# Two attention layers on one NeuronCore: the gated layer between them and the second attention merged into one block, with its first units interleaved, and the turned maxima spread by ScalarE in four scaled pieces

## The chip, the cores and the metric

The kernel runs on one core of a Trainium2 chip. The metric is the device time of one execution in microseconds (us), of which the median of several runs is quoted. A profile is one further execution taken with the hardware profiler. Engines: TensorE (PE; its weight loads are listed apart as PEld), VectorE (DVE), ScalarE (ACT), GpSimd (POOL) and the queue of SyncE (SP). Each works through its own list of instructions in order and meets the others at semaphores.

## What is computed

The input is 2048 tokens of 128 features. Two layers follow each other, each of the form `x = x + attention(norm(x)) * silu(ffn(norm(x)))`, all in fp32. What the change touches is the end of the first layer and the start of the second:

```python
x = x + s * g                       # end of layer 0
xn = _layernorm(x, axis=-1)
s = _L1_attn_ref(xn, W_Q, W_K, W_V, W_O, b_Q, b_K, b_V, b_O)   # 16 heads of 64, causal softmax
g = _silu(_L1_ffn_ref(xn, w_gate, w_up, w_down))               # silu(gate) * up, then down; int8 weights
x = x + s * g
```

Sequence and batch in the second attention: one sequence of 2048 tokens, 16 heads. The scores of a token are shifted by their row maximum before the exponential.

## The kernel before, in words

The program is a chain of blocks: loading and routing, the first attention, `between` (L1260) and `attention1` (L1536). A block ends with all engines meeting.

**Sizes.** Tokens are cut into 4 chunks of 512 (`C`) and 16 tiles of 128. PSUM has 8 banks of 128x512 fp32. The 16 heads of the second attention are done as 8 head pairs, each head on 64 of the 128 partitions.

**`between`** computes the gated layer of layer 1 and, at its start, finishes the last chunk of layer 0. For each chunk: `turn_xn` (L1316) transposes the normalised tokens, ScalarE copies them out twice (`take_xn`, L1396 and L1397: a rounded high part and the full one), VectorE takes the low part (`take_low`, L1459). `gate(c, f)` (L1333) is four matmuls for one third of the hidden columns; its number is n = 3c + f and it has one of two pairs of banks, so it waits for product n - 2. ScalarE does the Silu (L1404), VectorE the product (`multiply`, L1465), and `down(c)` (L1345) is 24 matmuls over the three products of the chunk, whose Silu ScalarE writes to `g` (L1412). Chunk 3 is late, since its tokens are the last of layer 0: its join (projection L1369, `join_sum`, moments, variance, a Sqrt on ScalarE L1392, `join_refine`, and on GpSimd `join_result` L380 to L384 and `join_normal` L390) runs beside the other chunks, twice a Sqrt between Silus. `down(3)` ends the block.

**`attention1`** is a fixed list of units, which PE fills and another engine takes out of its banks, in the same order on all queues (`fill` on PE, `take` on ScalarE and VectorE). Kinds of unit:
- project (L1780 to L1782): six matmuls to two banks, keys and queries of a head pair for a chunk. ScalarE writes the high parts with the bias (L1941, L1943), VectorE the low parts (L2016, L2020).
- maximum (L1806, L1811): a tile of 128 query rows against one chunk of keys, both heads, two banks. VectorE reduces each bank (L2030); after the last tile of a chunk a small reduction writes the negated maxima (L2037).
- turn (L1818): these maxima transposed, one bank. They are then spread into `max_rows` (L2044 on VectorE): each of the chunk's four tiles of columns is the turned 128x128 matrix times `own_tile`, which is one on the rows of that tile and zero on the others.
- scores (L1859, L1862): a chunk of queries against a tile of keys, both heads, with the maxima added by a matmul of ones against `max_rows`; the first scores of a chunk wait for its turn unit to be taken. ScalarE does the exponential, one instruction (L1968) where the two banks are neighbours, two (L1972) where they wrap round.
- value (L1793 to L1795), mix (L1840), total (L1828), bias (L1889).

Seven banks form a ring, given out in the order of the list, one or two at a time; a unit waits until the earlier owner of its bank has been taken. The eighth bank collects the weighted values (`weigh`, L1881). The list has 80 groups: each has four scores units with maximum tiles between them (counts in `MAXIMA`: 8, 6, 6, 8, 8 and then 2 to 5), after them the units of `STARTING` or `WHOLE` (projections, turns, values, mixes), then the total of a chunk that has ended, and last the four weighings of the group's scores. ScalarE copies a chunk's sum out (L1980), VectorE divides (reciprocal L2051, product L2054), and after the mix adds to the accumulator `attn` (L2103); in the last head pair it also multiplies by `g` and adds `x` (`finish`, L2006 and L2007). GpSimd sums the exponentials (L1763, L1765, L1769) and masks the diagonal (L1737).

In front of the groups stands `BEFORE`, one list for all engines:

```python
BEFORE = [("project", 0, 0), ("project", 0, 1)] + TILES[0:TC] + [("value", 0, 0), ("turn", 0, 0), ("bias", 0, 0)]
```

Before it the biases are turned (L1913), ScalarE copies them (L1931) and rounds the value weights (L1933), and GpSimd takes their low part (L1729), for which the value units wait. The bias unit is 16 matmuls; VectorE adds it to `row_o` (L2114) and spreads the row over all 16 tiles of `attn` (L2116), then starts the reductions of group 0.

## Time and profile before

| | us |
|---|---|
| median of 3 runs (lowest, highest) | 1384.57 (1384.45, 1385.58) |
| the profiled execution, its time | 1383.88 |
| its span, first to last instruction | 1381.9 |
| PE / DVE / ACT / POOL busy in the span | 1292.8 / 1024.9 / 755.8 / 691.7 |
| mean granted TensorE clock | 0.991 |
| start of `between` | 499.70 |
| last down projection of `between` | 531.99 |
| first scores of `attention1` | 547.74 |
| first weighing | 559.52 |

Dates are microseconds from the span's start. The clock is given as a share of the full 2.4 GHz; at 0.5 TensorE runs at 1.2 GHz. In a timeline row, several instructions of one kind are merged (x8), the second number is their time together, and the bracket says how long the engine had stood before and for whom. A group row gives the busy sum and the mean of one.

### The profile page before, as it was taken

What the parts mean: (1) busy time and instruction counts of PE and PEld (TensorE: products, weight loads), DVE (VectorE), ACT (ScalarE), POOL (GpSimd) and SP (SyncE); (2) the same over time, 40 slices, a digit from 0 to 9 for tenths busy, and PEclk for the clock granted to TensorE, in tenths of its full rate; (3) what the DMA queues carried; (4) which work ended last, traced back from release to release, by engine and by line L of the source; (5) the groups of instructions that cost most, each with busy time, mean ns of one, the idle gap of its engine ahead of it and who ended that gap; (6) DMA issues with size and microseconds to landing.
All of it is one profiled execution on the core that took longest, in us unless ns stands there. A gap on an engine that the chain in (4) does not pass through costs nothing. (4 is left out here: it accounts for less than half of the span.)

```text
span 1381.9 us, 26461 instructions
## 1 busy us (share of the span) xinstructions
PE 1292.8 (94%) x9840; PEld 677.4 (49%) x9840; DVE 1024.9 (74%) x1818; ACT 755.8 (55%) x1286; POOL 691.7 (50%) x528
## 2 busy tenths in 40 slices
PE   5889999999999987989999999999999999999897
PEld 3763222222222246555555655555655555655554
DVE  7667888888888875776766766766767766676868
ACT  6476777778887864344444444444444444444343
POOL 4101050100101111558787678777688787778771
PEclk9899999999999999999999999999999999999999
DMA  1522410000000000000000000000000000000000
GB/s 36 180 101 80 126 29 1 2 1 1 1 2 1 2 1 1 1 1 1 1 1 1 1 1 1 1 1 2 1 1 1 1 1 1 1 1 1 9 9 16
DMA packets 18172, 21.56 MB, mean 16 GB/s; under 512 B 7785, under 2 KB 15873, under 8 KB 16513
## 3 DMA queue, kind: packets, MB, share of 16 engines
q1 hardware_dynamic: 18048, 19.88, 4.5%
q8 instruction: 83, 1.36, 0.4%
q14 instruction: 41, 0.33, 0.1%
HBM read 14.63 MB, written 5.24 MB: 14 GB/s over the span
## 5 line engine op out<-in xcount | busy, mean ns | idle before, releaser
L1769 POOL TENSOR_TENSOR acc<-acc,prob 128x1024 f32<-128x1024 f32 (+3 forms) x250 | 493.8, 1975 | 87.0 <-ACT prob L1968 53.1
L2030 DVE TENSOR_REDUCE part_max<-psum 128x1 f32<-128x512 f32 (+3 forms) x640 | 352.8, 603 | 143.1 <-PE psum L1806 71.9
L1968 ACT ACTIVATE prob<-psum 128x1024 f32<-128x1024 f32 (+3 forms) x273 | 241.7, 896 | 285.7 <-PE psum L1862 279.9
L695 DVE TENSOR_SCALAR w<-psum 128x512 f32<-128x512 f32 x472 | 304.5, 686 | 59.3 <-PE psum L544 46.5
L644 ACT ACTIVATE w<-psum 128x512 f32<-128x512 f32 x552 | 293.9, 601 | 81.7 <-PE psum L544 81.3
L564 PE MATMUL psum<-w,v_cols 128*32 128x512 f32 x2048 | 274.0, 608 | 0.0
L1881 PE MATMUL psum<-prob,v_both 128*64 128x512 f32 (+3 forms) x1280 | 250.2, 533 | 0.6 <-POOL prob L1737 0.6
L1859 PE MATMUL psum<-q_hi,k_hi 64*128 64x512 f32 (+3 forms) x640 | 135.6, 408 | 32.0 <-DVE part_max L2030 17.7
L1881 PEld LDWEIGHTS psum<-prob,v_both 128*64 128x64 f32 x1280 | 87.7, 137 | 145.4 <-issue 134.6
L1806 PE MATMUL psum<-k_hi,q_hi 64*128 64x512 f32 (+3 forms) x640 | 135.7, 411 | 5.2 <-DVE part_max L2030 2.6
L1859 PE MATMUL psum<-q_lo,k_hi 64*128 64x512 f32 (+3 forms) x640 | 122.8, 364 | 0.0
L1862 PE MATMUL psum<-max_rows,ones_r 64*128 64x512 f32 (+3 forms) x640 | 122.6, 363 | 0.0
L1859 PE MATMUL psum<-q_hi,k_lo 64*128 64x512 f32 (+3 forms) x640 | 122.5, 363 | 0.0
L544 PEld LDWEIGHTS psum<-q_rows,k_rows 32*128 32x128 f32 x768 | 40.2, 181 | 153.9 <-ACT w L644 148.1
L2051 DVE RECIPROCAL inv<-psum 128x512 f32<-128x512 f32 x31 | 103.9, 3352 | 13.2 <-PE psum L1828 12.8
L380 POOL TENSOR_SCALAR xa<-xa,rstd_j,shift_j 128x128 f32<-128x128 f32 x16 | 6.9, 448 | 199.4 <-DVE shift_j L372 199.4
L1806 PEld LDWEIGHTS psum<-k_hi,q_hi 64*128 64x128 f32 x640 | 65.0, 184 | 83.0 <-issue 75.6
L1737 POOL TENSOR_SCALAR_AFFINE_SELECT prob<-prob 128x256 f32<-128x256 f32 x128 | 53.2, 423 | 97.6 <-ACT prob L1968 89.1
L544 PE MATMUL psum<-q_rows,k_rows 32*128 32x512 f32 x768 | 101.4, 493 | 0.1
L1859 PEld LDWEIGHTS psum<-q_hi,k_hi 64*128 64x128 f32 x640 | 65.9, 186 | 64.8 <-issue 49.4
L1765 POOL TENSOR_TENSOR acc<-prob 128x1024 f32<-128x1024 f32 x23 | 55.0, 2390 | 37.8 <-ACT prob L1968 32.3
L1972 ACT ACTIVATE prob<-psum 128x512 f32<-128x512 f32 (+3 forms) x94 | 45.5, 537 | 51.6 <-PE psum L1862 50.3
(310 smaller groups left out, 1486.4 us busy)
## 6 DMA issues: line engine op xcount, KB each, us to landing
q_rows<-q_dram SPq DMA_DIRECT2D x12, 256.0 KB
k_rows<-k_dram SPq DMA_DIRECT2D x3, 1024.0 KB
x<-in_L_attn_x SPq DMA_DIRECT2D x4, 256.0 KB, 3.8
mask<-in_L_ffn_attention_mask SPq DMA_DIRECT2D x1, 1024.0 KB, 5.9
q_dram<-x_high SPq DMA_DIRECT2D x1, 1024.0 KB, 6.9
q_dram<-x_low SPq DMA_DIRECT2D x1, 1024.0 KB, 6.9
k_dram<-q_rows SPq DMA_DIRECT2D x1, 1024.0 KB, 9.0
k_dram<-k_rows SPq DMA_DIRECT2D x1, 1024.0 KB, 6.2
```

The lines of the kernel that those rows point to most:

```text
L544: last = nc.tensor.matmul(pair_bank[n % RING][i], k_rows[group][rows, kt * P:(kt + 1) * P], q_rows[group][rows, qc * C:(qc + 1) * C], star ...
L564: last = nc.tensor.matmul(out_bank[turn % 2][h * VW:(h + 1) * VW, :], v_cols[group][:, kt, h, :], w[:, s % WR, h, :], start=(kt == 0), sto ...
L644: nc.scalar.activation(w[:, s % WR, 2 * m + i, :], pair_bank[n % RING][i], ACT.Relu)\
L695: nc.vector.tensor_scalar(w[:, s % WR, 2 * m + 1, :], pair_bank[n % RING][1], 0.0, None, ALU.max)\
L1769: nc.gpsimd.tensor_tensor(sums, sums, prob[:, s % PR, :, q0:C], ALU.add).then_inc(summed, 1)
L1806: last = nc.tensor.matmul(to[m][:, 0:n], q_hi[HALF[m], i * P:(i + 1) * P], k_hi[hp % 2][HALF[m], c * C:c * C + n], start=True, stop=not di ...
L1859: nc.tensor.matmul(to[m][:, q0:C], left[HALF[m], keys], right[HALF[m], at], start=n == 0, stop=False)
L1862: last = nc.tensor.matmul(to[m][:, q0:C], ones_r[HALF[m], :], max_rows[HALF[m], at], start=False, stop=True)
L1881: last = nc.tensor.matmul(out_bank[HALF[m], q0:C], v_pair[hp % 2][:, kt, HALF[m]], prob[:, s % PR, m, q0:C], start=kt == 0, stop=kt == (qc ...
L1968: last = nc.scalar.activation(prob[:, s % PR, :, q0:C], sh.psum[:, first:first + 2, q0:C], ACT.Exp, scale=SCALE)
L2030: free(nc.vector.tensor_reduce(part_max[:, m, i, c:c + 1], src[m][:, 0:cols], AX_X, ALU.max), unit, m)
L2051: free(nc.vector.reciprocal(inv[:, :], banks_of(unit)[0]), unit, 0)
```

## The change

The two blocks become one, `between_and_attention1`, with the buffers of the one laid over those of the other where they are free. Nine units that stood behind the block's end are put between the gates and down projections of the middle part, with fixed banks (`EARLY`): the bias unit (bank 3), projections (0,0) and (0,1), the first four maximum tiles (banks 2 and 3) and the first turn (bank 2). Only value unit (0,0) stays in `BEFORE`; the ring begins there at place 4. The turned biases go through bank 2 at the start, and the banks of the middle part are dealt out anew. VectorE's reductions and low parts, and ScalarE's high parts, stand in the matching places of their queues. The rounding of the value weights moves on ScalarE behind `take_xn(3)`. The spread of the bias row over `attn` moves from VectorE to GpSimd, behind the join and the last `turn_xn`, in front of the low value weights; value units wait for both, VectorE's groups for the spread. Last, `spread_maxima` of all 32 turn units moves from VectorE (one product of 128x512 with `own_tile`) to ScalarE (four copies of 128x128, each scaled by a column of `own_tile`).

```diff
-def attention1(nc, a, sh, out):
+def between_and_attention1(nc, a, sh, out):
...
-        BEFORE = [("project", 0, 0), ("project", 0, 1)] + TILES[0:TC] + [("value", 0, 0), ("turn", 0, 0), ("bias", 0, 0)]
+        EARLY = [(("bias", 0, 0), [3]), (("project", 0, 0), [2, 3])] + [(tile, [2, 3]) for tile in TILES[0:TC]] \
+            + [(("turn", 0, 0), [2]), (("project", 0, 1), [2, 3])]
+        BEFORE = [("value", 0, 0)]
         LAST = [("total", FINAL, None), ("mix", NP - 1, NC - 1)]
         HALVES = 2
-        UNIT = BEFORE + [u for k in range(GROUPS) for u in units_of(k)] + LAST
+        UNIT = [u for u, _ in EARLY] + BEFORE + [u for k in range(GROUPS) for u in units_of(k)] + LAST
         AT = {u: n for n, u in enumerate(UNIT)}
         WIDE = ("scores", "maximum", "project", "value")
         BANKS, EARLIER, FREED = {}, {}, {}
-        held, freed, place = [None] * RING, [0] * RING, 0
+        held, freed, place = [None] * RING, [0] * RING, 4
         for u in UNIT:
-            width = 2 if u[0] in WIDE or u == LAST[-1] else 1
-            BANKS[u] = [(place + i) % RING for i in range(width)]
-            place += width
+            if u in dict(EARLY):
+                BANKS[u] = dict(EARLY)[u]
+            else:
+                width = 2 if u[0] in WIDE or u == LAST[-1] else 1
+                BANKS[u] = [(place + i) % RING for i in range(width)]
+                place += width
             EARLIER[u] = [held[b] for b in BANKS[u]]
             for b in BANKS[u]:
...
-        q_hi = sb("q_hi", [P, S], F32R)
+        q_hi = sh.q_rows[1]
         q_lo = sb("q_lo", [P, S], F32R)
-        k_hi = [sb(f"k_hi{n}", [P, S], F32R) for n in range(2)]
+        k_hi = [sh.k_rows[1], sb("k_hi1", [P, S], F32R)]
         k_lo = [sb(f"k_lo{n}", [P, S], F32R) for n in range(2)]
         max_rows = sb("max_rows", [P, S], F32R)
-        v_both = sb("v_both", [P, 2, T, P])
+        v_both = sh.v_both
...
+        inner = prob[:, :, :, :].rearrange("p n m c -> p (n m c)").rearrange("p (f s) -> p f s", s=S)
+        act_gate = acc[:, 0, :, :]
+        wT = z[:, 0, 0:F1]
+        wT_int = k_hi[1][:, 0:2 * F1].rearrange("p (m f) -> p m f", f=F1)
+        w_real = v_both[:, 0, 0:3 * F1T, :].rearrange("p t d -> p (t d)").rearrange("p (m f) -> p m f", f=F1)
+        oT = v_both[:, 1, 0:TC, :].rearrange("p t d -> p (t d)")
...
+        gate_bank = [bank[4:6], bank[6:8]]
+        last_bank = bank[6 + TURN % 2]
+        ROWS_BANK = [0, 1, 2, 0]
+        JOIN_BANK = 3
+        DOWN_BANK = [0, 1, 1, RING]
...
             for b, earlier in zip(BANKS[unit], EARLIER[unit]):
                 if earlier is not None:
                     wait_bank(nc.tensor, earlier, b)
+                elif b == 0:
+                    nc.tensor.wait_ge(xnT_done, 4)
+                elif b in (1, 4, 5, 6):
+                    nc.tensor.wait_ge(inner_done, NC * F1T)
             return banks_of(unit)
...
+            link = Chain(pool, pool_step)
             nc.gpsimd.memset(neg_max[:, :, :, :], 0.0).then_inc(consts_set, 1)
+            pool.wait_ge(scaled_j, 1)
+            join_result(nc, link, sh, END, x_done)
+            pool.wait_ge(scaled_j, 2)
+            join_normal(nc, sh, END, normed)
+            pool.wait_ge(xn_turned, 4)
+            wait_freed(pool, ("bias", 0, 0))
+            nc.gpsimd.tensor_copy(attn[:, :, :], row_o[:, :].unsqueeze(1).to_broadcast([P, T, D])).then_inc(consts_set, 1)
             pool.wait_ge(bias_done, 2)
             nc.gpsimd.tensor_tensor(wv_low[:, :], sh.w_heads[:, 2, :, :].rearrange("p h d -> p (h d)"),
                                     wv_high[:, :].bitcast(F32), ALU.subtract).then_inc(consts_set, 1)
...
-                pe.wait_ge(consts_set, 2)
+                pe.wait_ge(consts_set, 3)
...
+            def turn_xn(c):
+                if c == 2:
+
+                    pe.wait_ge(bias_done, 1)
+                if c == END:
+
+                    pe.wait_ge(normed, 1)
+                    pe.wait_ge(finished, 1)
+                for j in range(TC):
+                    last = nc.tensor.transpose(bank[ROWS_BANK[c]][:, j * P:(j + 1) * P], sh.xa[:, c * TC + j, 0:D], sh.ident[:, :])
+                last.then_inc(xn_turned, 1)
...
+            gate(0, 0)
...
+            gate(0, 1)
+            gate(0, 2)
+            turn_xn(2)
+            pe.wait_ge(summed_j, 1)
+            fill(("bias", 0, 0))
+            gate(1, 0)
+            gate(1, 1)
+            pe.wait_ge(xnT_done, 3)
+            fill(("project", 0, 0))
+            gate(1, 2)
+            down(0)
+            for f in range(F1T):
+                gate(2, f)
+            fill(TILES[0])
+            down(1)
+            fill(TILES[1])
+            turn_xn(3)
+            fill(TILES[2])
+            down(2)
+            fill(TILES[3])
+            gate(3, 0)
+            gate(3, 1)
+            fill(("turn", 0, 0))
+            gate(3, 2)
+            fill(("project", 0, 1))
+            down(3)
             for unit in BEFORE:
                 fill(unit)
...
+            def spread_maxima(hp, c):
+                unit = ("turn", hp, c)
+                wait_filled(act, unit)
+                for j in range(TC):
+                    at = slice(c * C + j * P, c * C + (j + 1) * P)
+                    last = nc.scalar.activation(max_rows[:, at], banks_of(unit)[0][:, 0:P], ACT.Copy,
+                                                scale=own_tile[:, j, 0:1])
+                free(last, unit, 0)
...
+            activate(0, 0)
+            take_xn(1)
+            activate(0, 1)
+            activate(0, 2)
+            deviation(0)
+            take_xn(2)
+            activate(1, 0)
+            activate(1, 1)
+            split_high(0, 0)
+            activate(1, 2)
+            activate(2, 0)
+            finish_down(0)
+            deviation(1)
+            activate(2, 1)
+            activate(2, 2)
+            finish_down(1)
+            take_xn(3)
+            nc.scalar.copy(wv_high[:, :], sh.w_heads[:, 2, :, :].rearrange("p h d -> p (h d)")).then_inc(bias_done, 1)
+            activate(3, 0)
+            activate(3, 1)
+            take(("turn", 0, 0))
+            finish_down(2)
+            activate(3, 2)
+            split_high(0, 1)
+            finish_down(3)
...
-            def spread_maxima(hp, c):
-                unit = ("turn", hp, c)
-                at = slice(c * C, (c + 1) * C)
-                wait_filled(dve, unit)
-                free(nc.vector.tensor_tensor(max_rows[:, at].rearrange("r (j c) -> r j c", j=TC),
-                                             banks_of(unit)[0][:, 0:P].unsqueeze(1).to_broadcast([P, TC, P]),
-                                             own_tile[:, :, :], ALU.mult), unit, 0)
-
...
-            def spread_bias():
+            def add_bias():
                 unit = ("bias", 0, 0)
                 wait_filled(dve, unit)
-                dve.wait_ge(sh.second_loaded, SECOND)
                 free(nc.vector.tensor_tensor(row_o[:, :], row_o[:, :], banks_of(unit)[0][:, 0:D], ALU.add), unit, 0)
-                wait_freed(dve, unit)
-                link(nc.vector.tensor_copy(attn[:, :, :], row_o[:, :].unsqueeze(1).to_broadcast([P, T, D])))
...
+            take_low(0)
+            multiply(0, 0)
+            dve.wait_ge(projected, 1)
+            join_sum(nc, sh, END, bank[JOIN_BANK]).then_inc(summed_j, 1)
+            dve.wait_ge(summed_j, 1)
+            link(join_moments(nc, sh, sh.xa, END * TC, TC))
+            multiply(0, 1)
+            join_variance(nc, link, sh, 0, at_last, var_done)
+            take_low(1)
+            multiply(0, 2)
+            dve.wait_ge(root_done, 1)
+            join_refine(nc, link, sh, 0, at_last, scaled_j)
+            add_bias()
+            multiply(1, 0)
+            take_low(2)
+            multiply(1, 1)
+            multiply(1, 2)
+            dve.wait_ge(x_done, 1)
+            link(join_moments(nc, sh, sh.x, END * TC, TC))
+            join_variance(nc, link, sh, 1, at_last, var_done)
+            take(("project", 0, 0))
+            multiply(2, 0)
+            dve.wait_ge(root_done, 2)
+            join_refine(nc, link, sh, 1, at_last, scaled_j)
             dve.wait_ge(consts_set, 1)
+            take(TILES[0])
+            multiply(2, 1)
+            multiply(2, 2)
+            take(TILES[1])
+            take(TILES[2])
+            take_low(3)
+            take(TILES[3])
+            multiply(3, 0)
+            multiply(3, 1)
+            multiply(3, 2)
+            take(("project", 0, 1))
+            dve.wait_ge(consts_set, 2)
...
+            sh.v_both = sb0("v_both", [P, 2, T, D])
+            sh.v0 = sh.v_both[:, 0, :, :]
+
+            sh.v_cols = sh.v_both[:, 1, :, :].rearrange("p t (h v) -> p t h v", v=VW)
...
             attention0(nc, a, sh)
-            between(nc, a, sh)
-        attention1(nc, a, sh, out)
+            between_and_attention1(nc, a, sh, out)
```

## Rows read from the trace of the kernel before

**Rows 1.** Page, part 1: each engine's busy time, share of the span, instructions.

```profile
PE 1292.8 (94%) x9840; PEld 677.4 (49%) x9840; DVE 1024.9 (74%) x1818; ACT 755.8 (55%) x1286; POOL 691.7 (50%) x528
```

**Rows 2.** Windows from block start to first scores: length, busy by engine (instructions), PEclk, DMA.

```profile
499.70:535.80 36.10, 28.71 (x185) 23.90 (x185) 17.37 (x53) 22.25 (x36) 6.37 (x10) 1.00 0.00 0
535.80:547.40 11.60, 9.06 (x68) 7.21 (x68) 6.76 (x14) 6.01 (x9) 2.71 (x2) 1.00 0.01 3
```

**Rows 3.** Waits, 560 to 1340 us: waiter, releaser, us in total, times, longest.

```profile
PE psum L1859 <- DVE part_max L2030: 17.7, 23, 1.7
```

**Rows 4.** Timeline of the middle, PE: start, us, instruction, [idle before, releaser].

```profile
509.49 0.51 PE L1333 MATMUL psum<-x_high,wT_int 128*128 128x512 f32 x1 [1.69 <-DVE x_low L1459]
...
513.17 0.50 PE L1333 MATMUL psum<-x_high,wT_int 128*128 128x512 f32 x1 [1.55 <-DVE inner L1465]
...
531.99 2.94 PE L1345 MATMUL psum<-wT,inner 128*128 128x128 f32 x24 [1.41 <-DVE inner L1465]
```

**Rows 5.** Timeline of the middle: ScalarE, VectorE and GpSimd.

```profile
510.50 1.28 ACT L1404 ACT_TABLE_LOAD   x1
...
513.03 0.68 DVE L1459 TENSOR_TENSOR x_low<-xnT,x_high 128x512 fp32r<-128x512 f32 x1
513.04 1.72 POOL L383 TENSOR_TENSOR xa<-xa,g 128x512 f32<-128x512 f32 x1
```

**Rows 6.** Timeline from the block's end to the first weighing.

```profile
535.83 0.26 PEld L1913 LDWEIGHTS psum<-ident,bias_rows 8*128 8x128 f32 x3 [1.09 <-issue]
...
545.12 1.28 ACT L1968 ACT_TABLE_LOAD   x1
...
547.41 0.50 PE L1806 MATMUL psum<-k_hi,q_hi 64*128 64x512 f32 x2
...
547.84 1.23 DVE L2116 COPY xa<-row_o 128x2048 f32<-128x2048 f32 x1
...
549.10 8.05 DVE L2030 TENSOR_REDUCE part_max<-psum 128x1 f32<-128x512 f32 x16
...
550.44 0.45 PE L1859 MATMUL psum<-q_hi,k_hi 64*128 64x384 f32 x2
...
559.52 2.37 PE L1881 MATMUL psum<-prob,v_both 128*64 128x512 f32 x16
```

**Rows 7.** Groups by shape from 535 us: busy us, mean ns, idle before.

```profile
L1769 POOL TENSOR_TENSOR acc<-acc,prob 128x1024 f32<-128x1024 f32 x157 | 372.4, 2372 | 73.4 <-ACT prob L1968 53.1 <-ACT prob L1972 4.2 <-POOL acc L1765 0.4
...
L2051 DVE RECIPROCAL inv<-psum 128x512 f32<-128x512 f32 x31 | 103.9, 3352 | 13.2 <-PE psum L1828 12.8
...
L1941 ACT ACTIVATE k_hi<-psum,bias 128x512 fp32r<-128x512 f32 x32 | 22.0, 687 | 33.5 <-PE psum L1782 33.4
L2044 DVE TENSOR_TENSOR max_rows<-psum,own_tile 128x512 fp32r<-128x512 f32 x32 | 21.9, 683 | 13.7 <-PE psum L1818 13.7
...
L1980 ACT COPY z<-psum 128x512 f32<-128x512 f32 x32 | 18.8, 587 | 79.3 <-PE psum L1881 79.3
...
L1763 POOL COPY acc<-prob 128x1024 f32<-128x1024 f32 x8 | 8.3, 1037 | 0.0
...
L1729 POOL TENSOR_TENSOR wv_low<-w_heads,wv_high 128x1024 fp32r<-128x1024 f32 x1 | 2.4, 2399 | 1.3 <-ACT wv_high L1933 1.3
...
L1972 ACT ACTIVATE prob<-psum 128x128 f32<-128x128 f32 x8 | 1.8, 282 | 0.1
```

**Rows 8.** Timeline, PE, around 900 us: the weighing run of one group.

```profile
906.56 3.60 PE L1881 MATMUL psum<-prob,v_both 128*64 128x512 f32 x16
```

**Rows 9.** Timeline, last head pair, behind the first mix.

```profile
1308.46 2.18 DVE L2007 TENSOR_TENSOR xa<-xa,x 128x512 f32<-128x512 f32 x1
...
1311.38 0.50 PE L1859 MATMUL psum<-q_hi,k_hi 64*128 64x512 f32 x2 [2.79 <-DVE max_rows L2044]
```

**Rows 10.** Windows behind that wait: length, busy by engine, PEclk, DMA share, GB/s.

```profile
1310.00:1320.00 10.00, 8.62 (x54) 6.18 (x56) 7.48 (x13) 4.16 (x5) 5.89 (x5) 0.83 0.09 26
1313.00:1314.00 1.00, 1.00 (x10) 0.97 (x9) 0.60 (x2) 1.00 (x2) 0.00 (x0) 0.50 0.00 0
```

367 lines of the change are left out of this document (132 added, 235 removed).

## The prediction

> **What bounds the kernel now.** I read the page first: TensorE (PE) is busy 94% of a 1381.9 us span [rows 1], so only PE's waits can be won. The same execution took 1383.88 us and the median of the three runs is 1384.57, so 0.7 us is added to whatever the sum against this execution gives. Next the busy time by stage. From the start of the middle part (499.70) to its end (535.80) PE is busy 28.71 of 36.10 us, and from there to the first scores (547.40) 9.06 of 11.60 [rows 2]: 9.9 us of idle PE. The second attention behind it is nearly full: in its steady part PE waited 17.7 us for the row maxima and little else [rows 3].
>
> The timeline of the middle shows why PE stands: the first gate of a chunk waits for the low parts, the third for the product before last, a down projection for all its products [rows 4]. ScalarE carries that chain: a table load of 1.28 before each change between Sqrt and Silu [rows 5]. Behind the block's end PE loads its first weights 1.09 us late, and then the first projections, maxima, values, turned maxima and bias stand in one line before the first scores at 547.41 [rows 6].
>
> From then on VectorE (DVE) sets the pace of the first group: it spreads the bias row over the accumulator (547.84, 1.23) and only then starts its 16 reductions at 549.10, one run of 8.05 us. The first weighing matmul stands at 559.52 [rows 6].
>
> **The change part by part.** I walked the new order of each queue: an instruction starts at the latest of its queue's last issue and what it waits for, plus 0.04 to 0.05 us for the semaphore, with the durations of the timeline (gate 0.97, down projection 2.84, a maximum tile 0.3 to 0.5, product and low part 0.69 and 0.68, and so on; the longest stand in rows). The same walk of the old order ends at 531.9 for the last down projection (trace 531.99) and at 559.44 for the first weighing (trace 559.52) [rows 4, 6], so a date of it is good to some 0.1 us where the order is known.
>
> *Merged block with early units.* In the new order PE reaches the third transposition at 507.3 as before, and the bias matmuls (now 507.8 to 509.7) fill the wait for the low parts of chunk 1 that stood 1.69 [rows 4]. The first projection (six matmuls, 1.4) fills 511.7 to 513.1, where PE stood 1.55. After gate (2,2) come tile 0 (520.6), down 1, tile 1 (523.8), the transposition of chunk 3 (524.2; before 523.7), tile 2 (525.2, waiting 0.4 for DVE to free banks 2 and 3), down 2, tile 3 (528.4), gates (3,0) and (3,1), the turned maxima (530.9), gate (3,2), projection 1, and down 3 at 534.7 instead of 531.99. The whole costs down 3 2.7 us; in return all that stood behind it is done except one value unit (1.5) and one maximum tile. The first scores issue at 539.5, 7.9 us before 547.41.
>
> This agrees with the idle time: 9.9 us stood, the walk leaves some 2, in gate (0,2), gate (2,2), tile 2 and the spread in front of projection 1.
>
> *What is late next.* The exponential table is loaded only behind the value copies (before: 545.12 with the first scores filled after it, hidden [rows 6]). Now those copies end at 540.4, the load at 541.6, the first exponential at 542.7. Scores 1 share bank 1 with scores 0 and so wait until 542.7; before they issued at 550.44 behind a reduction [rows 6]. DVE has meanwhile done its pending tiles; from 544.1 it has ten reductions (5.4 by the sizes in its run of 16) plus the small maximum, then turn, value unit and first weighing at 551.6: **7.9 us gained** against 559.52. Behind this the order is the old one, and PE's waits there don't look back, so the gain stays.
>
> The Trainium skill (ScalarE: Activation LUTs, What ACT_TABLE_LOAD costs) gives a change of set some 2.66 us, a load and a drain of about the same length. Here the load took 1.28 and ScalarE went straight on [rows 5]; with the page's figure the gain would be 1.4 less.
>
> *Spread of the accumulator moved to GpSimd (POOL).* 128x2048 elements; nearest row below, POOL's copy of 1024 columns, 1.04, so 2.1; above, 4.7 by its addition of that width, 2.37 [rows 7]. It stands behind the last join and waits for the fourth transposition (524.8), and the subtraction for the low value weights is queued behind it (2.40 [rows 7]). Both ends leave them done by 532.1, and the value unit that waits for them starts at 537.6. DVE's group loop waits for the spread too, at 539. Cost nothing, under either end; only were POOL over 5 us longer would PE see it. DVE loses 1.23 on its way to the first reduction, already in the walk.
>
> *Turned maxima on ScalarE (ACT).* DVE loses 32 operations of 0.683 [rows 7]. A piece of 128 columns on ACT: 0.282 for an exponential of that size, plus the 0.100 by which the projection's copy with a per-partition operand (0.687) exceeds a plain copy (0.587) [rows 7], issued some 0.3 apart: 1.2 a turn, bounds 0.8 (pieces overlapping to 0.2) and 1.6 (no overlap). Queued behind the pieces on ACT are the z copy and the next group's exponentials. 31 of the 32 turns stand right in front of a group's weighing run, 3.60 us of PE in which ACT has nothing else but a split or that copy [rows 8]: nothing. If that cover went it would be 31 times 1.2. The turn in the middle is on the path, since projection 1 takes its bank: 0.4 against pieces of 0.2, already in the 539.5.
>
> What DVE's relief is worth: PE's 17.7 us for maxima come in groups after the total's reciprocal, 3.35 us [rows 7], and by the plan's lists turns (places 2, 5, 7, 9 of ten) and totals (0, 1, 3, 6) never share a group; the old spread ran in the weighing run, where DVE idles. So nothing of the 17.7, with one exception. In the last head pair the mix and two long products (the second 1308.46, 2.18) stood before the spread on DVE, and PE's scores waited 2.79 us until 1311.38 [rows 9]. On ACT the pieces are done by 1307; these scores issue at 1308.5, and the next ones wait for DVE's first reduction behind the products, at 1311.2 instead of 1312.7 (the old order at full clock): **1.5 us gained**.
>
> And right behind that wait the granted clock fell: 0.50 in the microsecond from 1313, that is 1.2 instead of 2.4 GHz, with PE busy throughout, and 0.83 in the mean from 1310 to 1320 [rows 10], so 0.17 x 10 = 1.7 us lost. PE had stood 2.8 us before it fell. In the new order it stands 1.6 there, and in the middle it stood 1.69 at a time and kept the full clock [rows 2, 4]. I take the **1.7 us** as won; bounds 0 and 1.7.
>
> The order of banks is shifted by four places; scores that wrap round the seven are done in two exponentials, and counting both plans gives 47 each: nothing.
>
> Sum: 7.9 + 1.5 + 1.7 = 11.1 against 1383.88, so 1372.8, and 1373.5 against the median.
>
> **The rivals.**
> 1. *The clock falls anyway, or elsewhere.* Gain 9.4 or a bit less: 1375.2. For it: that stretch keeps a wait of 1.6, since the reductions still stand behind two long products [rows 9]. Against: above.
> 2. *The early units get in their own way.* Banks 2 and 3 are single for six units, so a late reduction holds tile 2, tile 3, the turn, projection 1 and down 3 in turn. With DVE's low part of chunk 3 late: POOL's spread and subtraction run from 524.8 to 529.3 just when it is due (526.8). A DVE two-input sum took 2.18 with POOL running, where the low parts, a two-input form of the same shape, took 0.68 [rows 5, 9]. If it starts only when POOL is through (529.3) gate (3,0) issues 1.1 later, and so does all behind: 1374.6. With the first exponential or a further wait of that size, gain 6 to 8: 1377.
> The Trainium skill (SBUF — State Buffer, Who interferes with whom) makes this a rule: a VectorE instruction with two SBUF inputs and a GpSimd instruction that reads SBUF exclude each other for a whole instruction. By that rule, where the trace agrees only in part: beside DVE's low parts a POOL product took 1.72, while DVE lost nothing [rows 5].
> 3. *DVE's relief is worth more.* 31 times 0.61 against 17.7 us of waits for maxima [rows 3] would give up to 1356. Against: turns and reciprocals never share a group.
> 4. *Slower: ACT holds the turn too long.* If the pieces need another table than the exponential's, each of 31 turns pays two loads, 2.57 + 1.2 = 3.8 us. It decides from about 2.8, where the split or z copy (0.59) no longer fits in the 3.60 as well: (3.8 - 2.9) x 31 = 28, and 28 more than forecast is 1401.5. Against: projection copies and plain copies stand between exponentials, and one load is shown for the whole stage [rows 6].
> 5. *It doesn't do it:* that the units are early on the list and still start late. In the diff each stands between the gates and down projections as walked above, and in the same order on ACT and DVE, so this is only rival 2 in full: nothing won before the first weighing, 1381.
>
> **How the numbers follow.** Forecast 0.43; rival 1 0.18; rival 2 at 1374.6 (the exclusion alone) 0.15, in its larger form 0.12; rival 3 0.04; rival 5 0.04; rival 4 0.04. The measurement can tell 0.2%, 2.8 us, from no change, so all but rival 4 and a third of rivals 2 and 5 together lie below 1381.8: faster 0.91, same 0.05, slower 0.04. The range takes in gains of 6.5 to 13: 1371.5 (the forecast with PE's small gaps of 2 us in the middle filled as well) to 1378.0; outside are rivals 3, 4, 5 and the worst of 2.
>
> **What would show it.** First scores at 539 to 540; down 3 at 534 to 535; one exponential table load at 540.4 and scores 1 waiting for the first exponential; first weighing at 551 to 552; 128 pieces on ACT of 0.35 to 0.4 with no load between; POOL's spread near 524.8; no 2.8 us wait for the maxima's spread near 1300, full clock there; PE's waits for maxima still 15 to 19 us. I am wrong if the first weighing stands after 554, if table loads appear among the pieces, or if PE's waits for maxima fall by over 5 us.

## The result and the profile after

| | before | after |
|---|---|---|
| median of the timed runs (lowest, highest; runs), us | 1384.57 (1383.85, 1385.58; 5) | 1377.32 (1375.98, 1378.27; 5) |
| ratio after / before, 95% interval | | 0.9946 [0.9935, 0.9957] |
| the profiled execution, its time (its span), us | 1383.88 (1381.9) | 1376.82 (1374.9) |
| PE / DVE / ACT / POOL busy, us | 1292.8 / 1024.9 / 755.8 / 691.7 | 1294.0 / 1005.1 / 790.5 / 695.1 |
| mean granted TensorE clock | 0.991 | 0.988 |
| first copy of the block, first scores, first weighing, us | 499.70, 547.74, 559.52 | 501.07, 541.03, 554.34 |

The change gains 7.25 us by the medians, 0.5%; 11.1 were forecast. The page's first part answers to [rows 1]: TensorE has the same 9840 matmuls, its busy time is 1.2 us higher, and its mean clock is 0.003 lower.

```profile
PE 1294.0 (94%) x9840; PEld 678.0 (49%) x9840; DVE 1005.1 (73%) x1785; ACT 790.5 (57%) x1414; POOL 695.1 (51%) x529
```

Windows of the changed kernel, from the block's first copy to the first scores and from there to the first weighing (columns as in [rows 2, 10]: length, busy us of PE, PEld, DVE, ACT and POOL, granted clock, DMA share, GB/s):

```profile
501.07:541.03 39.96, 38.11 (x256) 31.14 (x258) 23.77 (x67) 27.04 (x47) 11.31 (x13) 1.00 0.00 1
541.03:554.34 13.31, 11.19 (x83) 8.69 (x79) 9.09 (x18) 6.36 (x11) 5.30 (x7) 0.74 0.01 1
545.70:552.50 6.80, 6.40 (x38) 4.87 (x37) 5.48 (x11) 1.51 (x4) 3.19 (x5) 0.50 0.01 2
```

Up to the first scores all is well: of 39.96 us PE stands 1.9, where it stood 9.9 in the two windows of [rows 2]. (Eight units moved in front, not nine as counted in the section on the change; the ninth of `BEFORE`, the value unit, stayed.) Behind them stands something new. The clock is granted at 0.74 in the mean, because for 6.8 us it is 0.50, which is 1.2 instead of 2.4 GHz. The timeline of the same stretch shows what came before:

```profile
541.03 0.39 PE L1673 MATMUL psum<-q_rows,k_rows 64*128 64x512 f32 x2
...
544.36 0.44 PE L1673 MATMUL psum<-q_rows,k_rows 64*128 64x384 f32 x2 [1.72 <-ACT prob L1895]
...
549.25 0.77 PE L1620 MATMUL psum<-k_rows,q_rows 64*128 64x512 f32 x2
...
554.34 1.94 PE L1695 MATMUL psum<-prob,v_both 128*64 128x512 f32 x10
```

The first scores issue at 541.03 (547.74 before). The second scores wait 1.72 for the first exponential, and 1.3 us behind that wait the clock falls. The pair of 512-column matmuls at 549.25 takes 0.77, against 0.50 for the same pair in [rows 6]. On ScalarE, as forecast, the table load (1.28, one in the stage, and none among the pieces) stands behind the value copies:

```profile
533.55 1.14 ACT L1908 ACTIVATE max_rows<-psum,own_tile 128x128 fp32r<-128x128 f32 x4
...
540.80 1.08 ACT L1878 COPY v_both<-psum 128x512 f32<-128x512 f32 x2 [0.78 <-PE psum L1609]
541.89 1.28 ACT L1895 ACT_TABLE_LOAD   x1
543.19 1.02 ACT L1895 ACTIVATE prob<-psum 128x1024 f32<-128x1024 f32 x1
```

In the last head pair, PE's timeline answers to [rows 9]: the wait of 2.79 for the spread is gone, and one of 1.66 for VectorE's reductions has taken its place, behind the two long products. ScalarE's four pieces (first row) are done before it.

```profile
1301.46 1.14 ACT L1908 ACTIVATE max_rows<-psum,own_tile 128x128 fp32r<-128x128 f32 x4 [0.81 <-PE psum L1632]
...
1306.99 0.50 PE L1673 MATMUL psum<-q_rows,k_hi 64*128 64x512 f32 x2 [1.66 <-DVE part_max L2018]
```

And a window around that wait:

```profile
1290.00:1310.00 20.00, 18.01 (x139) 11.26 (x137) 16.49 (x21) 8.28 (x14) 14.67 (x12) 1.00 0.05 14
```

It is at the full clock throughout, where [rows 10] had 0.83. PE's waits of the second attention, 560 to 1340 us, against the 17.7 of [rows 3]:

```profile
PE psum L1673 <- DVE part_max L2018: 20.7, 25, 1.7
PE psum L1673 <- ACT prob L1895: 8.1, 26, 0.8
```

VectorE's 19.8 us less of work shortened none of them; 20.7 is above the 15 to 19 that the forecast named.

**Where the 7.0 us between the two profiled executions lie**, by the dates of the first weighing matmul of a group (group 0, 5, 70, 72, 73) in the two timelines. The last column is the difference of the two intervals:

| stretch | before | after | gain |
|---|---|---|---|
| span's start to the block's first copy | 499.70 | 501.07 | -1.37 |
| block's first copy to group 0 | 59.82 | 53.27 | 6.55 |
| group 0 to 5 | 62.59 | 62.55 | 0.04 |
| group 5 to 70 | 662.89 | 663.52 | -0.63 |
| group 70 to 72 | 20.79 | 20.94 | -0.15 |
| group 72 to 73 (the wait of 2.79 and the half clock behind it) | 13.29 | 10.55 | 2.74 |
| group 73 to the end | 62.8 | 63.0 | -0.2 |

Four things had to be settled: what the 1.72 wait and the half clock of group 0 cost, where 0.8 us between groups 5 and 72 went, which part of the change gives the 2.74, and whether the 1.37 in front of the block, in code that the change does not touch, belongs to it.

### The profile page after: what moved, and what is told of

Read it like the earlier page. It is cut to its first block and busy times, and to the rows that moved or that the text cites. A ratio compares the mean times of both kernels' runs of the same rounds, so it can differ in the third digit from the quotient of the medians.

```text
span 1374.9 us, 26581 instructions
## 1 busy us (share of the span) xinstructions
PE 1294.0 (94%) x9840; PEld 678.0 (49%) x9840; DVE 1005.1 (73%) x1785; ACT 790.5 (57%) x1414; POOL 695.1 (51%) x529
## 5 line engine op out<-in xcount | busy, mean ns | idle before, releaser
L564 PE MATMUL psum<-w,v_cols 128*32 128x512 f32 x1536 | 204.1, 604 | 0.0
L1673 PE MATMUL psum<-q_rows,k_lo 64*128 64x512 f32 (+3 forms) x640 | 122.8, 364 | 0.0
L1673 PE MATMUL psum<-q_rows,k_rows 64*128 64x512 f32 (+3 forms) x320 | 68.3, 410 | 16.5 <-DVE part_max L2018 7.5
L1673 PE MATMUL psum<-q_rows,k_hi 64*128 64x512 f32 (+3 forms) x320 | 67.4, 405 | 17.5 <-DVE part_max L2018 13.3
L1620 PE MATMUL psum<-k_rows,q_rows 64*128 64x512 f32 (+3 forms) x320 | 67.9, 415 | 2.7 <-DVE part_max L2018 1.9
L564 PE MATMUL psum<-w,v_both 128*32 128x512 f32 x512 | 69.9, 619 | 0.0
L1676 PEld LDWEIGHTS psum<-max_rows,ones_r 64*128 64x128 f32 x640 | 65.9, 186 | 6.7
```

The lines of the kernel that those rows point to most:

```text
L564: last = nc.tensor.matmul(out_bank[turn % 2][h * VW:(h + 1) * VW, :], v_cols[group][:, kt, h, :], w[:, s % WR, h, :], start=(kt == 0), sto ...
L1620: last = nc.tensor.matmul(to[m][:, 0:n], q_hi[HALF[m], i * P:(i + 1) * P], k_hi[hp % 2][HALF[m], c * C:c * C + n], start=True, stop=not di ...
L1673: nc.tensor.matmul(to[m][:, q0:C], left[HALF[m], keys], right[HALF[m], at], start=n == 0, stop=False)
L1676: last = nc.tensor.matmul(to[m][:, q0:C], ones_r[HALF[m], :], max_rows[HALF[m], at], start=False, stop=True)
```

## The experiments

Below, "block" is the date of the block's first copy on ScalarE, and "to weigh 0" the time from there to the first weighing matmul. Each ratio is against the kernel before as timed beside that experiment (median 1385.28 us for experiments 1 to 4, 1384.67 for 5 and 6, 1384.42 for 7), so ratios and intervals of the traces compare better than medians.

**1. Only the spread of the maxima on ScalarE.** The kernel before, with `spread_maxima` of all turns moved as in the change:

```diff
-                free(nc.vector.tensor_tensor(max_rows[:, at].rearrange("r (j c) -> r j c", j=TC),
-                                             banks_of(unit)[0][:, 0:P].unsqueeze(1).to_broadcast([P, TC, P]),
-                                             own_tile[:, :, :], ALU.mult), unit, 0)
...
+                    last = nc.scalar.activation(max_rows[:, at], banks_of(unit)[0][:, 0:P], ACT.Copy,
+                                                scale=own_tile[:, j, 0:1])
+                free(last, unit, 0)
```

> The kernel before with only the turned maxima spread by ScalarE in four scaled pieces, nothing else. My theory (relief of VectorE shows at one place alone): first weighing at 59.8 us behind the start of the middle block as before, groups 1 to 71 as before within 0.5 us, and only between the weighings of groups 72 and 73 (13.3 us before) some 2.7 to 3.2 us less, with no half clock there; time 1381.5, about 3 less than before. Rival (VectorE's relief is worth something at every turn): the weighings draw ahead steadily through groups 10 to 70 and the time falls by 6 or more. Rival (the pieces cost ScalarE's readers): groups 1 to 71 lose 0.5 to 1 us, which would explain the 0.7 us that the changed kernel loses there.

Measured: 1381.47 us, ratio 0.9975 [0.9965, 0.9986]. To weigh 0: 59.76 (before 59.82). Group 72 to 73: 10.55, as in the changed kernel. The window around it is at the full clock:

```profile
1306.00:1316.00 10.00, 8.29 (x66) 5.48 (x66) 9.34 (x12) 5.31 (x10) 8.49 (x5) 1.00 0.09 26
```

So this part by itself gives all of the late pair's 2.74 us. The other stretches move by 0.35 at most, up and down: from the block's first copy to the end it takes 879.7 us instead of 882.2.

**2. Only the merged block.** The changed kernel, with the spread on VectorE again, in the middle too (diff of 1 the other way round, and `take(("turn", 0, 0))` from ScalarE's list to VectorE's, behind `multiply(3, 1)`):

```diff
-            take(("turn", 0, 0))
             finish_down(2)
...
             multiply(3, 1)
+            take(("turn", 0, 0))
             multiply(3, 2)
```

> The changed kernel with the turned maxima spread by VectorE again, in one product. My theory: all that the merge wins is there at the first weighing (53 us behind the block's start, as in the changed kernel, 59.8 before), and the 2.75 us between groups 72 and 73 are gone; time 1380. If the clock falls in the first group here too, the long wait of scores 1 for the first exponential is what goes with it. Rival (the loss of 0.7 us through groups 1 to 71 comes from the bank order shifted by four, not from ScalarE's pieces): it is here too.

Measured: 1379.84 us, 0.9957 [0.9943, 0.9970]. To weigh 0: 53.24, with the same half clock (547.2 to 554.0). In the last head pair the old wait is back, and yet the clock stays full there. PE's timeline, then two windows:

```profile
1309.50 0.50 PE L1673 MATMUL psum<-q_rows,k_hi 64*128 64x512 f32 x2 [2.80 <-DVE max_rows L2020]
```

```profile
1308.00:1318.00 10.00, 8.50 (x58) 5.15 (x60) 8.74 (x13) 4.10 (x4) 7.22 (x5) 1.00 0.09 26
1284.00:1294.00 10.00, 8.23 (x62) 6.44 (x58) 8.60 (x13) 4.69 (x5) 6.31 (x5) 0.83 0.00 0
```

Group 72 to 73 takes 12.00: 13.29 less the clock. This splits the 2.74: 1.29 for the clock, 1.45 for the wait. It also says that the gains of the two parts do not simply add, since each part alone had, in its one trace, no half clock in the last head pair. A half clock now stands some 22 us earlier, behind a wait of 1.7 that the traces of the kernel before and of the changed one have there too; there it costs 1.0 (group 70 to 71: 13.31, against 12.27 in the changed kernel's first trace). And the 0.6 us between groups 5 and 70 are there (663.47), so they belong to the merged kernel.

**3. The exponential's table earlier.** The changed kernel with an exponential of one column, whose result nobody reads, behind the last early down projection's Silu:

```diff
             finish_down(3)
+            nc.scalar.activation(warm[:, :], own_tile[:, 0, 0:1], ACT.Exp)
             for unit in BEFORE:
```

> The changed kernel with one exponential of a single column right behind the last Silu of the middle part, so that the exponential table is loaded before the value copies instead of behind them. My theory (TensorE's wait of 1.72 us for the first exponential in group 0, and the half clock of 6.8 us right behind it, are what kept the merge from giving 7.9): the first exponential starts near 41.2 us behind the block's start instead of 42.1, the wait falls to 0.8, the clock stays full, first weighing at 52 instead of 53.2, time 1375.5. Rival (the clock falls there by its own course, whatever the wait): wait shorter by 0.9, half clock as before, 0.5 us won at most. Rival (VectorE's reductions set group 0 anyway): first weighing unchanged.

Measured: 1375.58 us, 0.9928 [0.9916, 0.9941]. The timeline of ScalarE, that of PE, and two windows:

```profile
538.94 1.28 ACT L1964 ACT_TABLE_LOAD   x1
540.24 0.20 ACT L1964 ACTIVATE warm<-own_tile 128x1 f32<-128x1 f32 x1
540.35 1.05 ACT L1879 COPY v_both<-psum 128x512 f32<-128x512 f32 x2
541.29 1.04 ACT L1896 ACTIVATE prob<-psum 128x1024 f32<-128x1024 f32 x1
```

```profile
542.47 0.44 PE L1674 MATMUL psum<-q_rows,k_rows 64*128 64x384 f32 x2 [0.52 <-ACT prob L1896]
```

```profile
542.00:551.50 9.50, 7.62 (x67) 5.75 (x69) 8.14 (x16) 4.63 (x12) 5.25 (x7) 1.00 0.01 2
1280.00:1290.00 10.00, 8.05 (x58) 6.48 (x56) 7.88 (x14) 4.27 (x5) 7.04 (x5) 0.83 0.00 1
```

The load is hidden beside the value unit, the wait falls from 1.72 to 0.52, the clock stays full in group 0, and the first weighing stands 51.11 behind the block's first copy instead of 53.27. From the second scores to the weighing it is 8.60, against 9.98 in the changed kernel: 1.4 for the half clock and the reductions behind it, and the other 0.8 for the late table. That the clock stays full here is not one lucky trace: the four traces with the early table (experiments 3, 5, 6 and 7) all have a wait of 0.52 and the full clock in group 0, and the five timed runs of this experiment have a mean granted clock of 0.990, those of the changed kernel 0.986 to 0.989. The time as such is not parted from the changed kernel's by the intervals of the ratios ([0.9916, 0.9941] and [0.9935, 0.9957]); the first weighing is, 2.2 us earlier where such intervals repeat to 0.1. Near 1285 a half clock stands, where the changed kernel's first trace has none; group 70 to 71 takes 13.50, against 12.26 in experiment 6, which has none there: 1.2 us.

**4. The spread in sixteen pieces.** The changed kernel with pieces of 32 columns, the same work in four times as many instructions:

```diff
                 for j in range(TC):
+                    for q in range(4):
+                        at = slice(c * C + j * P + q * 32, c * C + j * P + (q + 1) * 32)
```

> The changed kernel with each piece of 128 columns cut into four of 32, so 16 instructions for a turn, about 3.3 us of ScalarE instead of 1.14 (0.285 a piece measured, less 96 columns). The walk says that a turn is free up to about 2.8 us because it stands in front of the weighing run, and costs about 0.7 us for each 1 us beyond, with 31 turns: time 17 us longer, 1394, range 8 to 25. Rival (ScalarE is far from the path in the whole stage, with 43% of the span idle): no change but 2 us in the middle part. Rival (it is on the path already): 31 times 2.2, 68 us longer.

Measured: 1385.38 us, 1.0003 [0.9994, 1.0012], by the two ratios 7.9 above the changed kernel. A turn on ScalarE beside PE's weighing run (all sixteen weighing matmuls), first in group 9, then in group 7:

```profile
657.21 2.37 PE L1695 MATMUL psum<-prob,v_both 128*64 128x512 f32 x16
...
657.85 0.68 ACT L1870 ACTIVATE q_rows<-psum,bias 128x512 fp32r<-128x512 f32 x1
...
658.42 2.95 ACT L1910 ACTIVATE max_rows<-psum,own_tile 128x32 fp32r<-128x32 f32 x16
...
661.13 0.72 ACT L1918 COPY z<-psum 128x512 f32<-128x512 f32 x1
```

```profile
638.33 3.65 PE L1695 MATMUL psum<-prob,v_both 128*64 128x512 f32 x16
...
638.44 2.95 ACT L1910 ACTIVATE max_rows<-psum,own_tile 128x32 fp32r<-128x32 f32 x16 [0.67 <-PE psum L1632]
```

PE's waits, 560 to 1340:

```profile
PE psum L1673 <- DVE part_max L2020: 20.0, 25, 1.7
PE psum L1673 <- ACT prob L1895: 9.6, 26, 0.7
PE psum L1673 <- ACT max_rows L1910: 2.8, 7, 0.4
```

A turn is 1.81 us longer on ScalarE, 56 over 31 turns; group 5 to 70 grows by 8.45 to 671.97. The dates of the weighings say where. The growth is 0.62 to 0.68 us in each of 13 groups (places 2 and 9 of every ten: 9, 12, 19 and so on to 69), and at most 0.05 in any other. In group 9 the weighing run is 2.37 us long, a projection's high parts stand in front of the pieces and the copy of `z` behind them, and ScalarE is through 2.3 us behind the run's end. In group 7 the run is 3.65 long and covers all. Group 12 has the short run too, with the `z` copy behind the pieces; group 15 has it as well, but its pieces start 0.76 us before the run and cost nothing. So in 13 groups the cover ends near 2.3 us a turn (2.95 less 0.65, an estimate that takes each further us to cost one), and in the other turns it lies above 2.95. The expectation had 17 us, range 8 to 25, and the measured growth is at its low end; but by its own rule (0.7 for each us beyond 2.8, 31 turns) its 3.3 us give only 10.9, and the 2.95 measured give 3.3, so the number was met without the mechanism. At 1.14 there is room everywhere. This trace's group 0 has the same wait of 1.72 as the changed kernel and kept the full clock: second scores to weighing 8.75, against 9.98. (Of its ten timed runs seven have a mean clock of 0.992, as this trace, and three 0.987 to 0.989.)

**5. The ring begun where it used to.** Experiment 3's kernel with one more edit:

```diff
-        held, freed, place = [None] * RING, [0] * RING, 4
+        held, freed, place = [None] * RING, [0] * RING, 0
```

> The kernel with the early table, and the ring of banks begun at place 0 instead of 4, so that from the first group on every unit has the banks that it had in the kernel before. My theory (the 0.6 to 0.8 us that all three merged kernels lose between the weighings of groups 5 and 70, and the spread alone does not, comes from the shifted banks: which scores wrap round and are done in two exponentials): the loss is gone, groups 5 to 70 within 0.2 of the kernel before, 0.7 us less than the kernel with the early table alone. Rival (it comes from the other buffers or from the addresses of the merged block): the loss stays at 0.6 to 0.8.

Measured: 1374.55 us, 0.9923 [0.9909, 0.9936]. Group 5 to 70: 663.03, where experiment 3 has 663.60 and the kernel before 662.89. No half clock stands near 1285, as this window shows, nor in group 0:

```profile
1284.00:1294.00 10.00, 9.06 (x60) 5.35 (x62) 8.88 (x14) 3.11 (x4) 7.20 (x4) 1.00 0.00 1
```

In groups 5 and 70 themselves the spread on ScalarE moves 0.3 us back and forth, so the fairer stretch is group 5 to 72: 683.7 in the kernel before and 683.7 in experiment 1, 684.5 in the changed kernel and in experiment 6, 683.8 here and 684.0 in experiment 7. Of the 0.8 that the merged kernel loses, 0.5 to 0.6 came from the shift of the banks by four places; the rest stays with the merged block.

**6. The long products later.** Experiment 3's kernel, with the first output block's two long products on VectorE (`finish(0)`, [rows 9]) moved out of the mix to the end of group 74:

```diff
-                    finish(qc)
+                    if qc:
+                        finish(qc)
...
+                if k == GROUPS - 6:
+                    finish(0)
```

> The kernel with the early table, and the two long products by which VectorE finishes chunk 0 in the last head pair moved from right behind the mix of group 72 to the end of group 74, where VectorE idles. My theory (with the spread gone the reductions behind these two products are what TensorE still waits for there): weighing 72 to weighing 73 takes 9.0 us instead of 10.55, and the rest keeps its length, so 1.5 us less than the kernel with the early table. Rival (the 1.5 comes back in group 74 or 75, where the products now stand): nothing at weighing 76.

Measured: 1373.90 us, 0.9919 [0.9907, 0.9932]. Group 72 to 73: 8.93 instead of 10.55; at group 76 0.4 of that is given back (35.47 from 72, against 36.71), so 1.2 is kept. PE's waits from 1298 to 1345 in the changed kernel, then in this one:

```profile
PE psum L1673 <- DVE part_max L2018: 2.4, 2, 1.7
PE psum L1642 <- ACT prob L1895: 1.2, 1, 1.2
```

```profile
PE psum L1643 <- POOL acc L1584: 1.2, 1, 1.2
PE psum L1674 <- DVE part_max L2020: 0.9, 1, 0.9
```

**7. All three.** Experiments 3, 5 and 6 in one kernel. (The ring is that of the PSUM banks, as in experiment 5; the expectation below calls it one of `prob` buffers.)

> The changed kernel with the three edits together: the one-column Exp behind the last early down projection, the ring of prob buffers begun at place 0, and the first output block's finish moved to the end of group 74. Theory: the three act in different places (first scores; the bank order of groups 5 to 70; group 76), so their gains add. From the run with the early Exp alone (0.9928 of the kernel before): the ring is worth 0.6 us more (drift of 0.70 against 0.13 us between groups 5 and 70), the late finish 1.2, together 0.9928 - 1.8/1384.6 = 0.9915, some 1372.8 us if the kernel before takes 1384.6. Rival: the finish and the ring move the same bank turns of the last groups, and only the larger shows: 0.9919, as with the late finish alone.

Measured: 1373.70 us, 0.9917 [0.9903, 0.9930]. The times alone do not part 0.9915 from 0.9919. The traces say that the gains nearly add: from the block's first copy to the end it takes 870.2 us, 0.3 less than in experiment 6 and 1.0 less than in 5, and 1.4 less than in experiment 3 without that one's half clock, where 1.8 were expected; group 5 to 70 663.19, 72 to 73 8.98. By its median it is the fastest of the kernels run here, not parted from experiment 6 by the intervals, but parted from the changed kernel (0.9946 [0.9935, 0.9957]) and 4.2 us shorter than the changed kernel's mean of 874.4 from the block on.

**8. Both kernels profiled again**, for their dates: the changed one twice, the one before twice.

> The changed kernel once more, for the places of its half clock. The changed kernel's profile began the middle block at 501.07 and the kernel with VectorE's spread at 502.70, against 499.7 to 500.0 in all others; both had a half clock of 13.65 us near the start instead of 10.24. If that is chance, this look may begin at 499.9. If it belongs to the kernel it begins at 501 again. In the same way: half clock behind scores 1 in group 0, or not (the kernel with sixteen pieces had the same wait of 1.72 and kept the clock).

> As the look before, for the same question: block start at 499.9 or 501.1, and whether the clock is halved in group 0 behind a wait of the same 1.7 us.

> The kernel before, once more, for its dates alone. Two traces of code with its first stage have the block's first copy at 499.7 and 499.9 us; of merged kernels two have 500.0 and six 501.1 to 502.7. If the later start is chance, this one can also have 501 to 503; if it belongs to the merged kernels, 499.7 to 499.9. The two theories also part on TensorE's half clock near 35 us: 10.2 us long with the early start, 13.7 with the late one.

> The same kernel before a second time, with the same two theories: a block start at 501 to 503 us with a half clock of 13.7 us near 35 us would say chance; 499.7 to 499.9 with 10.2 us again would leave it with the merged kernels, or with chance still, at lower odds.

The four took 1378.25, 1379.30, 1385.08 and 1385.65 us. With all others ("block to end" is the span less the block's date; of the half clocks those between 500 and 1360 us are given, by the microsecond in which they start):

| kernel | block | to weigh 0 | groups 5 to 70 | groups 72 to 73 | block to end | half clock |
|---|---|---|---|---|---|---|
| before, three traces | 499.70, 500.68, 501.79 | 59.82, 59.83, 59.79 | 662.89, 662.86, 662.81 | 13.29, 13.28, 13.30 | 882.2, 882.3, 881.9 | 1312, 1313, 1314 |
| after, three traces | 501.07, 501.61, 502.57 | 53.27, 53.24, 53.28 | 663.52, 663.50, 663.49 | 10.55, 10.54, 10.55 | 873.8, 874.7, 874.7 | 546; 546, 1287; 547, 1288 |
| 1 spread only | 499.90 | 59.76 | 662.61 | 10.55 | 879.7 | none |
| 2 merge only | 502.70 | 53.24 | 663.47 | 12.00 | 875.9 | 547, 1288 |
| 3 early table | 499.96 | 51.11 | 663.60 | 10.55 | 872.8 | 1285 |
| 4 sixteen pieces | 499.95 | 53.88 | 671.97 | 10.54 | 882.9 | none |
| 5 and old ring | 502.17 | 51.34 | 663.03 | 10.55 | 871.2 | none |
| 6 late finish | 502.29 | 51.27 | 663.54 | 8.93 | 870.5 | none |
| 7 all three | 501.05 | 51.40 | 663.19 | 8.98 | 870.2 | none |

Within one kernel the intervals up to group 73 repeat to 0.1 us, and only the block's date, the half clocks and the last 60 us move. The kernel before itself starts its block anywhere from 499.70 to 501.79:

```profile
501.79 0.59 ACT L1415 COPY o_sb<-psum 128x512 f32<-128x512 f32 x1 [1.86 <-PEq L417]
```

So the 1.37 us in front of the block, in the two traces compared above, is within what the unchanged code does by itself. Over three traces each the means are 500.7 and 501.8; whether the change moves that mean at all stays open. From the block's first copy to the end, where the change acts, the means are 882.1 and 874.4: 7.7 us.

## Why the prediction was right, and where its size was wrong

**The order of the middle: right.** The walk had the first scores 39.8 us behind the block's first copy (499.70 to 539.5); they stand at 39.96. (The 547.41 that the prediction sets against them is a maximum tile's row [rows 6]; the first scores of the kernel before stood at 547.74, so the gain there is 8.1 rather than 7.9.) Down 3 was walked at 35.0 and stands at 35.4 (536.44), the load at 40.7 and stands at 40.8. Second scores waiting for the first exponential, no wait for GpSimd's spread: as said. The first weighing was walked 7.9 us earlier and is 6.55 earlier. The step that failed is the last one, "from 544.1 it has ten reductions ... first weighing at 551.6": it reckoned PE at the full clock. The new wait in front was in the walk ("wait until 542.7"), and what it did to the clock was not. Experiment 3, which shortens that wait, has the full clock and 8.60 us instead of 9.98; experiment 4, with the wait and the full clock, has 8.75. With 8.75 in place of 9.98 the first weighing would stand 52.04 behind the block's first copy, 7.8 less than 59.82.

**Two of its own signs came out against it.** "I am wrong if the first weighing stands after 554": it stands at 554.34, and at 554.85 and 555.85 in the later traces. Of that, 1.4 to 2.9 us lie in front of the block, where unchanged code varies; counted from the block's first copy the limit was 54.3 and the weighing stands at 53.3, still 1.4 later than walked. And the waits for maxima are 20.7, not 15 to 19: of the rise of 3.0 some 1.7 is the wait that took the place of the spread's 2.8 in the last head pair, and 0.9 lies between groups 5 and 70 (below). The measured time lies 0.7 inside the slow end of the range and 3.8 from the forecast. It is the 1377 of rival 2's larger form, but by luck: the late low part on which that rival rests did not occur.

**"It stood 1.69 at a time and kept the full clock": the argument that was too weak.** I used it to say that a wait of 1.6 is harmless. In group 0 the clock fell behind 1.7 in four traces of five, and near 1287 behind 1.7 in two traces of the changed kernel out of three. Rival 1, that the clock falls anyway or elsewhere, is what happened. It had 0.18, and its time of 1375.2 held one half clock, where two traces of three have two.

**The late head pair: right in place, a bit smaller.** 1.5 forecast for the wait, 1.45 found (experiment 2 against the changed kernel); 1.7 for the clock, 1.29 found. The 1.4 us that PE stood in those 10 us [rows 10] are no reason, since they lie in front of the half clock, as a window of the kernel before over the half clock alone shows:

```profile
1312.07:1315.48 3.41, 3.41 (x24) 3.00 (x22) 1.12 (x3) 1.35 (x3) 0.57 (x1) 0.50 0.13 38
```

The working, 0.17 x 10, takes every matmul to be twice as long at half clock. In that stretch 512-column matmuls start 0.43 apart (1313.62, 1314.05, 1314.48) where behind it they start 0.23 apart, so somewhat less than twice; that this makes up the whole 0.4 is not shown.

**"The order of banks is shifted ...: nothing" was wrong.** The merged kernel loses 0.6 us from group 5 to 70 and 0.15 more to group 72, and 0.5 to 0.6 of that goes with the ring begun at 0 (experiments 5 and 7). I had counted the exponentials cut in two, which are equal (94 instructions in every trace), and no other effect of the order. Which wait the ring moved stays open: between groups 5 and 70 the waits for maxima are 15.5 to 15.6 us before and in experiment 1, 16.4 in the changed kernel and in experiment 2, and still 16.3 in experiments 5 and 7, so their rise belongs to the merged block and not to the ring.

**The table load.** By the Trainium skill (ScalarE: Activation LUTs, What ACT_TABLE_LOAD costs), a change of set costs some 2.66 us, half of it a drain. The trace does not agree in this place: from the load's start to the exponential's it is 1.30 (541.89 to 543.19), and 1.30 again in experiment 3 (538.94 to 540.24). The measurement decides; by the page's figure the second scores would have come 1.4 later.

**GpSimd and VectorE.** The low part of chunk 3, on which rival 2 rested, took 0.68 at 528.51, just when GpSimd's spread ended:

```profile
526.68 1.89 POOL L1541 COPY xa<-row_o 128x2048 f32<-128x2048 f32 x1 [1.40 <-PE psum L1715]
528.75 2.71 POOL L1543 TENSOR_TENSOR wv_low<-w_heads,wv_high 128x1024 fp32r<-128x1024 f32 x1 [0.18 <-ACT wv_high L1955]
```

```profile
528.51 0.68 DVE L1980 TENSOR_TENSOR x_low<-xnT,x_high 128x512 fp32r<-128x512 f32 x1
```

The spread took 1.89 (taken 2.1, bounds 2.1 and 4.7: a little below the lower one). The Trainium skill (SBUF — State Buffer, Who interferes with whom) has a VectorE instruction with two SBUF inputs and a GpSimd instruction that reads SBUF exclude each other, and the order of issue decide which of them waits. These rows agree with that: the low part issued first and lost nothing, and GpSimd's subtraction, which started 0.24 into it, took 2.71 against 2.40 in [rows 7]. So do [rows 5], where the low part issued 0.01 before the product that took 1.72; the prediction read them as agreeing only in part. Rival 2 needed the low part to come behind both GpSimd instructions. It came between them, and only 0.06 us of it lay beside the spread, so these rows do not test what a low part issued during the spread would have paid.

**The pieces on ScalarE: right.** 1.2 a turn was taken, 1.14 measured, and between groups 5 and 72 nothing of it shows (683.7 in the kernel before and in experiment 1). Rival 4's point of decision, about 2.8 for all 31 turns, is not: it took every weighing run for 3.60 us [rows 8]. Experiment 4 shows runs of 2.37 us, and a cover that ends near 2.3 in 13 groups and above 2.95 in the others. Its formula, (2.95 - 2.9) x 31, gives 1.6 us where 8.45 were found.

**The relief of VectorE: right.** 19.8 us of its work gone, and the waits for maxima did not fall (15.5 before, 15.6 in experiment 1 and 16.4 after, between groups 5 and 70).

In all, against the forecast of 11.1: 1.2 for the half clock in group 0, 0.1 in the walk, 0.5 in the late pair, 0.8 between groups 5 and 72, 0.2 behind group 73 (it is there in experiment 1 too), and over three traces 0.7 for the half clock near 1287 (two of three, 1.0 each). That leaves 7.6; the traces show 7.7 from the block on, and the medians 7.25.

## What to carry to other kernels

When a stage is tightened, look up the next wait in the new order, and what stands in front of it on the other engine: here the activation table's load, hidden before, came onto the path, and one tiny exponential in an idle place hid it again, for 2.2 us at the first weighing. When work is hidden behind another engine's run, take the shortest such run in the plan: here it was 2.37 us, not the 3.60 of the forecast. A half clock that a change removes in one place may turn up behind the next wait, so its gain needs a rival of its own in the forecast. Compare two kernels by intervals within the stretch that was changed, and take a second trace of the old kernel before a date in front of that stretch is explained.

## What the runs showed of the hardware that I had not expected

- **The half clock is not tied to one wait.** Behind the same wait of 1.7 in group 0 the clock fell to 1.2 GHz for 6.8 us in four traces (the changed kernel three times, experiment 2) and stayed at 2.4 in experiment 4. Behind 2.8 in the last head pair it fell in three traces of the kernel before and not in experiment 2. Behind 1.7 near 1287 it fell in four of thirteen traces. What decides between them was not found; each half clock in the second attention cost 1.0 to 1.3 us.
- **Scaled copies overlap.** Four copies of 128x128 with a per-partition scale, 0.36 to 0.42 each, take 1.14 together, so they start some 0.25 apart; sixteen of 128x32, 0.34 in the mean, take 2.95. A quarter of the columns saves a tenth of the time of one. Groups by shape from 535 us, the changed kernel and experiment 4:

```profile
L1908 ACT ACTIVATE max_rows<-psum,own_tile 128x128 fp32r<-128x128 f32 x124 | 35.5, 375 | 8.2 <-PE psum L1632 8.2
```

```profile
L1910 ACT ACTIVATE max_rows<-psum,own_tile 128x32 fp32r<-128x32 f32 x499 | 92.3, 343 | 8.2 <-PE psum L1632 8.2
```

- **The start of this program varies by itself.** A half clock near 35 us lasts 10.2 or 13.7 us in the same kernel, and the instruction that ScalarE starts at 52.7 us in the first trace of the kernel before comes 0.8 and 1.9 later in the other two, of 1.0 and 2.1 at the block's first copy. Windows of the second and third trace of the kernel before, from 33 to 49 us:

```profile
33.00:49.00 16.00, 10.85 (x176) 10.80 (x177) 11.98 (x37) 9.70 (x17) 7.53 (x14) 0.68 0.36 113
```

```profile
33.00:49.00 16.00, 10.27 (x167) 10.21 (x168) 11.87 (x36) 10.26 (x17) 8.12 (x15) 0.57 0.33 98
```
